# A tuned mixture-of-experts kernel on TensorE: two halves' Gram products move behind the first tile's products, the slot map streams 117 columns in place of 39, and filler products stand in three places of the routing

## The reference

```python
ys = cond * 256 ** -0.5
d = rsqrt(einsum('bi,io->bo', ys * ys, W * W) + 1e-8)
y = einsum('bsi,io->bso', x * ys[:, None, :], W) * d[:, None, :]
lang = softmax(y @ lang_w.T + lang_b)                      # 4 languages
router = y @ router_w.T + router_b + 0.1 * expert_weights(lang)
top_p, top_i = top_k(softmax(router), 2);  top_p /= top_p.sum(-1)
h = gelu(einsum('bsd,edh->bseh', y, w1) + b1)
expert_out = einsum('bseh,ehd->bsed', h, w2) + b2
out = x + sum_k top_p[k] * expert_out[top_i[k]]
```

## Time and profile before

| | us |
|---|---|
| three runs | 302.35, 305.21, 306.31 |
| their median | 305.21 |
| the profiled execution | 302.91 |
| its span, first to last instruction | 301.2 |
| PE, PEld, DVE, ACT, POOL busy | 277.1, 230.9, 202.7, 196.0, 169.1 |
| mean granted TensorE clock | 0.961 |

### The profile page before, as it was taken

One profiled execution on the slowest core, in us unless ns is written; L12 is line 12 of the kernel. 1 busy time (PEld: TensorE's weight loads), 2 busy tenths in 40 slices (PEclk: granted clock), 3 DMA queues, 4 the chain that ended last, 5 costly groups with the idle time before them and its releaser, 6 DMA issues.

```text
span 301.2 us, 9047 instructions
## 1 busy us (share of the span) xinstructions
PE 277.1 (92%) x3103; PEld 230.9 (77%) x3103; DVE 202.7 (67%) x459; ACT 196.0 (65%) x425; POOL 169.1 (56%) x159
## 2 busy tenths in 40 slices
PE   7899967999999999999999999999999999999800
PEld 5778967688899998888888888888888878887500
DVE  3956785799999997665665765765756665756510
ACT  3446369499897997576566666666665766675500
POOL 8100036800878668767667667667677567655330
PEclk9799977899999999999999999999999999999985
DMA  6799995599764224232322322422422322412220
GB/s 163 305 400 381 359 291 163 179 351 413 264 181 73 38 39 69 41 71 38 56 56 38 58 54 38 62 50 38 68 40 41 70 39 39 72 21 23 32 33 1
DMA packets 24104, 35.72 MB, mean 119 GB/s; under 512 B 4144, under 2 KB 19968, under 8 KB 23904
## 3 DMA queue, kind: packets, MB, share of 16 engines
q1 hardware_dynamic: 16544, 24.75, 23.7%
q0 software_dynamic: 7488, 10.39, 21.0%
q10 hardware_dynamic: 32, 0.01, 0.0%
HBM read 27.61 MB, written 9.64 MB: 124 GB/s over the span
## 4 chain that ended last, share of the span: by engine, by line
PE 84%; DMA 7%; POOL 1%; DVE 1%; issue 1%; SPq 1%; ACT 0%; DVEq 0%; POOLq 0%
PE ps L611 35%; PE ps L628 29%; PE ps L511 5%; PE ps L529 4%; PE ps L620 4%; PE ps L603 3%; DMA out<-onehot,idx 3%; DMA wsp<-in_L_ffn_w 3%; DMA wsp<-in_x 2%; PE ps L593 1%; SPq L340 1%; PE ps L484 1%; PE ps L493 1%; DVE wsp L862 1%; POOL out L442 1%
## 5 line engine op out<-in xcount | busy, mean ns | idle before, releaser
L611 PE MATMUL ps<-onehot,wsp 128*128 128x128 f16 x1872 | 157.1, 219 | 0.1
L788 ACT ACTIVATE pay<-ps,cur 128x128 f32<-128x128 f32 x312 | 117.2, 462 | 59.2 <-issue 42.2
L611 PEld LDWEIGHTS ps<-onehot,wsp 128*128 (+1 forms) x1872 | 131.6, 96 | 31.4 <-issue 0.3
L628 PE MATMUL ps<-wsp,pay 128*128 (+1 forms) x616 | 138.5, 314 | 1.2 <-DVE pay L1072 1.2
L442 POOL DMA_INDIRECT out<-onehot,idx x39 | 73.0, 1871 | 19.6 <-POOL onehot L433 10.4
L1072 DVE SCALAR_TENSOR_TENSOR pay<-pay,cur 128x512 f16<-128x512 f32 x72 | 54.9, 763 | 28.5 <-ACT pay L776 27.2
L433 POOL TENSOR_SCALAR onehot<-onehot,cur 128x256 f32<-128x256 f32 x37 | 37.9, 1025 | 55.2 <-DVE onehot L1090 37.0
L416 POOL DMA_INDIRECT rows<-y_rows,idx x39 | 44.4, 1137 | 13.4 <-issue 11.6
L628 PEld LDWEIGHTS ps<-wsp,pay 128*128 128x128 f16 x616 | 48.4, 96 | 3.6 <-issue 1.6
L1066 DVE TENSOR_SCALAR pay<-pay,cur 128x512 f16<-128x512 f32 x36 | 20.3, 565 | 27.6 <-ACT pay L788 27.6
L776 ACT ACTIVATE pay<-pay,cur 128x512 f16<-128x512 f32 x36 | 26.0, 722 | 1.2
(11 more groups left out here) (176 smaller groups left out, 215.1 us busy)
## 6 DMA issues: line engine op xcount, KB each, us to landing
stage<-in_L_ffn_w SPq DMA_DIRECT2D x9, 1024.0 KB, 10.3
wsp<-in_L_ffn_w SPq DMA_DIRECT2D x7, 1024.0 KB, 11.6
y_rows<-pay SPq DMA_DIRECT2D x4, 512.0 KB, 9.5
wsp<-in_x SPq DMA_DIRECT2D x3, 512.0 KB, 8.3
b2bc<-in_L_ffn_b SPq DMA_DIRECT2D x1, 1024.0 KB, 7.7
rows<-y_rows,idx POOLq DMA_INDIRECT x39, 3.0
out<-onehot,idx POOLq DMA_INDIRECT x39, 4.0
wsp<-in_x SPq DMA_DIRECT2D x2, 256.0 KB, 5.6
```

The lines of the kernel that those rows point to most:

```text
L611: last = mm(ps[:, HB + (2 * j + g) % RING, c * P:(c + 1) * P], wsp[:, bass.ds(e, 1), o:o + P].rearrange("p a f -> p (a f)"), xsp[:, j % RI ...
L628: last = mm(ps[:, OB + j % 2, 0:width], hsp[:, (2 * j + g) % NH, part, c, :], wsp[:, bass.ds(e, 1), o + w:o + w + width].rearrange("p a f ...
L788: last = a.activation(to, ps[:, HB + (2 * j + g) % RING, c * P:(c + 1) * P], ACT.Gelu, bias=cur[:, j % CURS, cc:cc + 1], scale=cur[:, j % ...
```

## The change

Four edits, on two engines.

On TensorE, `keep_warm(5, 1, 512)` is put ahead of the wait for `picked` (five filler products of 512 columns into bank 1; a wait for `lg_read` stands ahead of them), and `keep_warm(4, 1, 512)` between `gram(2)` and `sum_squares(2)`. The six filler products behind the slot map become eight (`WARM`), with other operands (ones in place of the one-hots).

The slot map's moving operand is read three times over (a broadcast dimension of 3), so that each of its 32 matmuls writes 117 columns; only the first 39 are read afterwards.

`gram(3)` moves from between the slot map and the filler products to behind tile 0's up products, and `sum_squares(3)` from there to behind the first half of tile 1's up products.

On VectorE, `gram_max(3)` moves from ahead of `split_low(0)` to behind the table of tile 1, and `scale_weights(3)` from there to behind `split_low(4)` in the main loop's first round.

```diff
-WARM = 6
+WARM = 8
...
             sum_squares(0)
+            pe.wait_ge(lg_read, T)
+            keep_warm(5, 1, 512)
...
             gram(2)
+            keep_warm(4, 1, 512)
             sum_squares(2)
...
-                    last = mm(ps[:, MB, 0:NT], ohv[:, :, c], tilehot[:, :, c], start=(c == 0), stop=(c == K * T - 1))
+                    last = mm(ps[:, MB, 0:3 * NT].rearrange("p (a n) -> p a n", a=3), ohv[:, :, c],
+                              tilehot[:, :, c].rearrange("p (a n) -> p a n", a=1).broadcast_to([P, 3, NT]), start=(c == 0),
+                              stop=(c == K * T - 1))
             last.then_inc(mapped, 1)
-            gram(3)
-            for _ in range(WARM):
-                mm(ps[:, RB, :], ones[:, :], onehot[:, 0:512], start=True, stop=True)
+            keep_warm(WARM, 1, 512)
...
             blocks((0, 1), None)
-            sum_squares(3)
+            gram(3)
             pe.wait_ge(te_ready, 1)
...
+                if j == 0:
+                    sum_squares(3)
...
             gelu_table(0, 3)
-            gram_max(3)
             split_low(0)
             expert_table(0)
             split_low(2)
             expert_table(1)
-            scale_weights(3)
+            gram_max(3)
             for j in range(NT):
...
                 for n in LOWS.get(2 * j + 1, ()):
                     split_low(n)
+                if j == 0:
+                    scale_weights(3)
```

## The result

The changed kernel takes 310.09 us (median of 6 runs, 309.07 to 312.35), the kernel before 304.93 us beside it: a ratio of 1.023, interval 1.018 to 1.028 (this ratio is not the quotient of the two medians, which is 1.017). The change is slower by some 5 to 7 us, where I had forecast none that can be measured. Run once more beside other runs of before (e12), it gave 1.024, interval 1.019 to 1.029.

A forecast was written before the change was run, and what follows sets the result against it. PE, busy for 224.0 of 225.0 us from 60 to 285 us, was taken as the bound. Terms −2.16 + 1.83 + 0.3 + 0 + 1.65 = +1.62 us on 302.91 gave 304.5 us, no measurable change; range 301.4 to 308.4.

The forecast's parts named there:

- 117 columns in place of 39: Slot map, on the path to index and gathers: extra columns hide under the weight load, 0; far end +5.2 us.
- the map pays by the column: Rival: the map's 32 products cost up to 5.2 us more through strided moving columns, 309.7 us; chance 0.10.
- a map of over 3.5 us: Sign that the forecast is wrong: the slot map's 32 products were expected to keep 0.08 us each.
- Gram products leave the wait: Group 3's Gram products no longer stand between slot map and fillers: up products begin at 54.65, not 56.81, −2.16 us.
- They come back behind tile 0: The same 32 Gram products run behind tile 0, where PE has no idle time to hide them: +1.83 us.
- Filler behind group 2: Four fillers ahead of `sum_squares(2)` end 0.3 us late and delay the slot map: +0.3 us, from 0 to +1.1.
- ahead of `picked`: Five fillers, 1.07 us, fit into PE's idle 2.31 us ahead of the counting products: cost 0.
- The clock at the first up products: After some four nearly idle microseconds, up products begin at the lower clock for 3.3 us: +1.65 us, ends 0 and 3.3.
- VectorE and ScalarE: Main loop: VectorE's splits come 2 to 3 us later, covered by 3 us of slack before down products: 0, at most +1.

The follow-up runs named there:

- e12: The changed kernel run again unchanged, beside other runs of the kernel before; 311.14 us, ratio 1.024.
- e6: The kernel before with 78 columns in the slot map in place of 39; a single execution, 304.03 us.
- e3: The changed kernel with `tilehot` laid out so that the 39 columns of one product are neighbours in memory; 315.87 us, ratio 1.044.
- e4: The kernel before with only group 3's Gram products and VectorE's two steps moved, 39 columns, six fillers, no new ones; 306.51 us, ratio 1.014.
- e9: As e4, but VectorE's split of half 0 waits until GpSimd has put out its second gather; 307.00 us, ratio 1.013.
- e5: As e4, with 10 fillers behind the slot map in place of 6 and 4 more between the transposes of tiles 0 and 1; 304.03 us, ratio 1.000.
- e7: As e4, with VectorE's split of half 0 written as four instructions instead of one; 306.75 us, ratio 1.011.
- e10: Kernel before with VectorE's changed order, group 3's Gram products left in the wait, 3 fillers behind them, 7 between tile 0 and 1 transposes; 303.89 us, ratio 0.998.

## Why the prediction was wrong

**117 columns in place of 39, priced at 0: the step that failed.** I chose between 0 and +5.2 by the Gram row, whose 128 columns pass in 0.057 us, and by the slow weight load. But those moving columns stand 4 bytes apart, the map's 64. Measured: 0.213 us a product, +4.19 us, 1.7 ns for each column (e6) and 0.098 with neighbours even at the lower clock (e3). My argument against the rival, that 39 columns explain 0.082 only if the load is free, was nearly what is the case: 39 × 1.7 is 0.066, which leaves 0.016. The rival "the map pays by the column" gave 309.7 us, and the measured time is 310.1. It had the mechanism; that the number fits so closely is in part luck, since its 5.2 us for the map were 1.0 too many and the other terms, 1.6 in all, came to 3.2. The map's 6.81 us are also one of my signs of being wrong, "a map of over 3.5 us". I had given the rival 0.10, and the range ended at 308.4, below it. What I said of this end was wrong too: 308.4 lies 3.9 us above the forecast, which is three quarters of the map's price and not a fourth. The Trainium skill (SBUF — State Buffer, "Door 1: The DMA port swizzle") says that reads keep their full rate only while successive elements fall in the same 16-byte line, 8 of them at bfloat16's size at the most, and pay for each new line. That rule speaks against the widened product, and I had not weighed it; the trace agrees, with 4-byte steps free (128 columns in 0.057 us) and 64-byte steps at 1.7 ns. Two ends 5 us apart with no row like the new operand deserved a far larger chance and a range that held both.

**Gram products leave the wait, −2.16.** The direction was right, the size was −0.93 in e4. Missing was that the split of half 0, moved forward, now runs beside the second gather's instruction, which is held by it: 1.82 us instead of 0.97 (e4, e9). It stood in the trace of before: the fourth gather there took 2.36 us beside this very split. Of the remaining 0.4, 0.2 is the second pair of transposes at the lower clock (0.48 us from its start to the up products, before 0.25), and 0.2 that I had put the landing too early. The Trainium skill (SBUF — State Buffer, "SBUF: two separate sides") says that GpSimd cannot write the descriptors of a DMA while VectorE runs certain operations that take the port pair which the two share, as a lock held for the whole instruction. I hadn't weighed it. The runs agree that the gather's instruction stands still beside the split.

**They come back behind tile 0, +1.83.** The term was right: 1.83 in the changed kernel, 1.84 in e4. The move without filler in the wait is a loss, as e4 shows against before. With the wait filled (e5, ratio 1.000) its cost is seen in the rows, and no longer in the time.

**Filler behind group 2, +0.3; ahead of `picked`, 0.** The clock stayed full under group 2's Gram products in the changed kernel, the four fillers took 0.9 us, and the map started at 45.94: 0. What set that start was VectorE's first piece of one-hots, for which PE waited 0.79 us; before, the map had followed `sum_squares(2)` without a wait. That the filler ahead of `picked` kept the clock up isn't shown: without it the clock was full there too in e5.

**The clock at the first up products, +1.65.** Right in kind: it fell at about 59.1 after PE's idle time, as before's trace and the Trainium skill (TensorE: Matmul & The Clock Gate, Part 1) had it. The size is 1.11, since it had fallen a microsecond before the up products began. e5 shows that filler in that wait takes the term away.

**VectorE and ScalarE, 0 to +1.** Measured: 1.1 in the first profile of the changed kernel, just above the ceiling, but 0.3 in e12, the same kernel, and 0.3 in e4. So most of it isn't a price of the change that returns each time. Of the 1.1, 0.2 is a wait for VectorE's maximum of a later group, which e4 has too, and 0.65 comes at tile 6. For tile 6 the first profile shows this: VectorE now waits for group 3's Gram products before it splits half 4, as its timeline in the changed kernel shows; behind this split stand on SyncE's queue two weight loads and the copy of x into the output, and behind the copy GpSimd's first scatter and the gather of tile 6 (DVE, SP and the chain of waits):

```profile
66.06 0.42 DVE L898 TENSOR_REDUCE wsum<-ps 128x2 f32<-128x256 f32 x1 [5.38 <-PE ps L529]
66.40 2.34 DVE L915 SCALAR_TENSOR_TENSOR wsp<-stage,wscale,wsp 128x2048 f16<-128x2048 f32 x1
```

```profile
68.77 1.62 SPq L320 DMA_DIRECT2D stage<-in_L_ffn_w  x2
70.44 1.55 SPq L350 DMA_DIRECT2D out<-in_x  x2
```

```profile
71.11 13.53 DMA out<-in_x
...
85.48 3.19 POOL out L442
88.67 0.31 issue
88.97 6.98 DMA rows<-y_rows,idx
95.95 0.04 issue
96.00 0.44 PE ps L606 x2
```

PE waits 0.52 us for these rows at 96.00. In e12 GpSimd's first scatter doesn't wait for the copy, and PE doesn't wait at tile 6:

```profile
86.95 1.66 POOL L442 DMA_INDIRECT out<-onehot,idx  x1 [0.31 <-POOL onehot L433]
```

I had followed the late splits to the down products, and not down SyncE's queue. That this queue is the cause in the first profile was read from the chain, not tried.

**In sum:** the terms come to −0.8 (from index to first up product: 6.81 us, before 7.64) + 4.2 + 1.1 + 1.8 + 1.1 = 7.4 us of span in the first profile, where I had 1.6. The medians lie 5.2 us apart, since the profiled execution of before was 2.0 us under its median and that of the changed kernel was not.

## What to carry to other kernels

Before widening a matmul to keep TensorE's clock up, look at how far apart its moving columns stand: filler on operands that don't step costs nothing here, filler inside a strided product cost 4 us on the path. Filler belongs where the engine will idle just before dense work, in this kernel the wait for the gathers, and not where it idled before light work. Work that fills a wait should not be moved out of it to shorten a chain, if behind the wait its engine is the bound: the rows here show 1.8 us paid for that, of which the time showed nothing once the wait was filled.

## What the runs showed of the hardware that I had not expected

- Moving columns of float16 that stand 64 bytes apart pass in 1.7 ns each, and as slowly at 2.4 as at 1.2 GHz (0.213 and 0.214 us a product of 117); side by side, 117 pass in 0.098 us at 1.2 GHz.
- VectorE's write of 1248 float16 elements took 0.81 us side by side and 5.5 us when each stood 78 bytes from the one before.
- GpSimd's instruction for an indirect gather, 0.97 us alone, ended 0.83 to 0.86 us after VectorE's split had ended wherever the two overlapped for long (1.82, 2.21 and 3.02 us in e4, e7 and e9), and a run of four short instructions held it like one long one. The 1.18 us one, which had begun just ahead of the split, was not held.
- The clock's state in the first 20 us goes with a shift of the whole run by some 2.5 us: in e12 it was low from about 7.4 to 17.7, before from 7.9 to 11.3, and the counting products began at 42.80 against 40.26. In e10, whose list up to there is that of the kernel before, it was low from 8.1 to 18.3, and they began at 43.03. I take this for much of the scatter of the kernel before, which was not tried.
